# A gated cross-attention and mixture-of-experts block: VectorE's expert selection split over two slots, its one-hot products a slot later, TensorE's rank matmuls behind the queries

## What is computed

```python
x = x + tanh(g_xattn) * xattn(layernorm(x), ctx, mask, ...)
x = x + tanh(g_ffn) * ffn(layernorm(x), ...)
# in ffn, per token:
scores = sigmoid(h @ gate_w.T)                 # 32 experts
sc = scores + e_bias
group_scores = top_k(sc.reshape(T, 8, 4), 2)[0].sum(-1)
# the 4 best of 8 groups are kept, the scores of the others set to 0
masked = where(score_mask > 0, sc, 0.0)
topk_idx = top_k(masked, 6)[1]
topk_w = scores at topk_idx, / their sum, * 2.5
out = sum over the 6 experts of topk_w * relu2(h @ up[e].T) @ down[e].T
      + relu2(h @ shared_up.T) @ shared_down.T
```

## Time and profile before

| | us |
|---|---|
| median of 3 runs | 762.55 |
| lowest and highest | 761.95 to 765.81 |
| the profiled execution, its own time | 763.1 |
| its span in the trace | 761.3 |
| TensorE busy | 704.7 (93%) |
| VectorE busy | 521.1 (68%) |
| ScalarE busy | 454.3 (60%) |
| GpSimd busy | 490.4 (64%) |

### The profile page before, as it was taken

How to read it: one execution, slowest core, us unless ns; L and a number is a source line. 1 busy time by engine, 2 the same in 40 slices (tenths; PEclk the granted TensorE clock), 3 DMA queues, 4 the chain that set the end, 5 groups by cost and what they waited for, 6 DMA issues and landing times.

```text
span 761.3 us, 17715 instructions
## 1 busy us (share of the span) xinstructions
PE 704.7 (93%) x5360; PEld 600.2 (79%) x5360; DVE 521.1 (68%) x1782; ACT 454.3 (60%) x1299; POOL 490.4 (64%) x532
## 2 busy tenths in 40 slices
PE   5978898999899999889996999999999999999977
PEld 4867797888788888775672889988898878988865
DVE  0867578787778787876471445556578878888783
ACT  0267576778787878764414455567655665566730
POOL 1244442566666666578888857777777777777772
PEclk9999999999999999999999999999999999999999
DMA  8970000144222222435659566665699999999865
GB/s 310 376 226 2 1 3 1 67 143 150 92 90 91 90 92 95 155 134 201 220 184 285 166 202 213 189 186 185 206 322 320 324 319 339 313 332 340 263 213 164
DMA packets 78237, 144.72 MB, mean 190 GB/s; under 512 B 13750, under 2 KB 60097, under 8 KB 77120
## 3 DMA queue, kind: packets, MB, share of 16 engines
q1 hardware_dynamic: 51472, 67.46, 28.4%
q0 software_dynamic: 19968, 52.34, 18.6%
q10 hardware_dynamic: 6704, 23.80, 9.7%
HBM read 78.00 MB, written 69.73 MB: 194 GB/s over the span
## 4 chain that ended last, share of the span: by engine, by line
PE 50%; DVE 16%; POOL 12%; issue 5%; DMA 5%; ACT 5%; DVEq 5%; ACTq 1%; SPq 0%; POOLq 0%
PE ps L1427 10%; PE ps L1412 10%; POOL routed_rows L446 9%; PE ps L1400 5%; PE ps L1212 4%; PE ps L1222 4%; PE ps L1308 4%; DMA mid<-routed_rows 3%; ACT att L533 3%; PE ps L1166 3%; POOL bias_o L440 3%; PE ps L1112 2%; PE ps L1298 2%; PE ps L1199 2%; DMA picked<-in_mask 2%
## 5 line engine op out<-in xcount | busy, mean ns | idle before, releaser
L446 POOL DMA_INDIRECT routed_rows<-x_n,slots x120 | 120.1, 1001 | 64.7 <-issue 27.7
L483 POOL DMA_INDIRECT token_parts<-hid,place x112 | 114.2, 1020 | 45.1 <-issue 28.3
L629 ACT ACTIVATE att<-ps 128x512 f32<-128x512 f32 x106 | 63.3, 597 | 108.8 <-PE ps L1400 101.0
L1427 PE MATMUL ps<-big,att 128*128 x448 | 119.7, 390 | 8.9 <-ACT hid L653 3.3
L1412 PEld LDWEIGHTS ps<-att 128*128 128x128 f32 x848 | 112.2, 193 | 5.6
L1412 PE MATMUL ps<-att 128*128 128x128 f32 x848 | 112.6, 276 | 0.0
L1427 PEld LDWEIGHTS ps<-big,att 128*128 128x128 f32 x448 | 78.9, 191 | 29.3 <-issue 22.4
L533 ACT ACTIVATE att<-ps,nmax,rstd 128x154 f32<-128x154 f32 x176 | 82.0, 494 | 13.3 <-DVE nmax L758 13.1
L1212 PE MATMUL ps<-att,big 128*64 128x128 f32 x1024 | 70.7, 281 | 16.7 <-ACT att L550 11.7
L642 ACT ACTIVATE att<-big 128x256 f32 x224 | 80.2, 408 | 1.7 <-issue 0.8
L1212 PEld LDWEIGHTS ps<-att,big 128*64 128x64 f32 x1024 | 60.0, 138 | 24.4 <-ACT att L550 14.2
(11 more groups left out here) (254 smaller groups left out, 1439.1 us busy)
## 6 DMA issues: line engine op xcount, KB each, us to landing
mid<-routed_rows SPq DMA_DIRECT2D x224, 138.0 KB
big<-token_parts ACTq DMA_DIRECT2D x19, 768.0 KB, 6.9
x_n<-token_parts ACTq DMA_DIRECT2D x9, 768.0 KB
routed_rows<-pad_row SPq DMA_DIRECT2D x1, 4416.0 KB, 23.2
routed_rows<-pad_row SPq DMA_DIRECT2D x32, 138.0 KB, 2.8
x_all<-in_x SPq DMA_DIRECT2D x4, 1024.0 KB, 14.0
big<-in_x_t SPq DMA_DIRECT2D x4, 1024.0 KB, 16.1
big<-in_w_moe SPq DMA_DIRECT2D x2, 2048.0 KB, 11.4
```

The source lines that it names most:

```text
L446: nc.gpsimd.indirect_dma_start(rows, bass.IndirectOffsetOnAxis(ap=slots[:, t, k:k + 1], axis=0), normed(t), None).then_inc(s_sca[t // TB % ...
L483: nc.gpsimd.indirect_dma_start(parts, bass.IndirectOffsetOnAxis(ap=place[:, p // 2 % 8, p % 2 * 2 + j:p % 2 * 2 + j + 1], axis=0), y_sb[p ...
L629: A.activation(xt(p), ps[:, p % 2, :], ACT.Copy).then_inc(s_xts, 1)
L1427: ins = M(ps[:, 6 + p % 2, j * D:(j + 1) * D], h_t[:, p % 2, j * P:(j + 1) * P], w_exp[:, bass.ds(e, 1), 256:512].rearrange("p a n -> p (a ...
```

## The change

VectorE's selection is cut in two behind the removal of the group maxima. `router_top_groups` (the first half) stays in slot 4b+8 in front of `invert`. `router_select` (the second half, from `chosen` to `sel`) moves to slot 4b+9, behind that slot's maxima and its residual add, which comes ahead of it. `router_pick` (the products `hot` and `picked`) moves out of `router_slots` to slot 4b+10, behind that slot's maxima and ahead of its residual add. On TensorE `ranks` moves behind the remaining transposes and the queries. The last block's router, which runs behind the slots, keeps its order. No instruction is added or removed.

```diff
-            def router_select(b):
+            def router_top_groups():
                 for i in range(TB):
                     V.max(best[:, i, :], group_2[:, i, :])
...
                     V.match_replace(group_r[:, i, :], best[:, i, :], group_2[:, i, :], -2.0e38)
+
+            def router_select():
                 dve.drain()
                 V.tensor_tensor(chosen, group_r[:, :, 0:NG], group_2[:, :, 0:NG], ALU.not_equal)
...
+
+            def router_pick():
                 V.tensor_tensor(hot[:], key[:].unsqueeze(2).broadcast_to([P, TB, TOPK, NE]),
...
+                if T % 4 == 2 and T >= 10:
+                    router_pick()
                 if T % 4 == 0 and T >= 8:
                     residual_add(T - 3)
                     router_groups()
+                if T % 4 == 1 and T >= 9:
+                    residual_add(T - 3)
+                    router_select()
...
                 if T >= 3:
-                    if T % 4 or T < 8:
+                    if T % 4 > 1 or T < 8:
                         residual_add(T - 3)
...
                 if T % 4 == 0 and T >= 8:
-                    router_select((T - 8) // 4)
+                    router_top_groups()
...
-                if T % 4 == 1 and T >= 9:
-                    ranks((T - 9) // 4)
                 if 2 <= T < NT + 2:
                     probs_t(T - 2, 1)
                     probs_t(T - 2, 2)
...
                     ins = queries(T + 2)
...
+                if T % 4 == 1 and T >= 9:
+                    ranks((T - 9) // 4)
```

More of the change, by code:

```diff
@@ L978, in _ @@
             router_groups()
-            router_select(7)
+            router_top_groups()
+            router_select()
             add_shared(1, 0)
             router_slots(7)
+            router_pick()
             router_weights(7)
```

## The result

| | us |
|---|---|
| changed kernel, median of 4 runs | 777.66 (772.99 to 788.11) |
| kernel before, median of 4 runs | 763.14 (761.95 to 765.81) |
| ratio, with its 95% interval | 1.0123 (1.0074 to 1.0172) |
| the profiled execution of the changed kernel | 788.11, span 786.3 |
| TensorE, VectorE, ScalarE, GpSimd busy | 714.5, 520.6, 454.8, 487.1 |

By the ratio the changed kernel is 1.2% slower, some 9.4 us; the medians stand 14.5 us apart. Predicted were 4.2. The side was right, the size was not: 777.66 lies above the range of 761.5 to 770.5.

A forecast was written before the change was run, and what follows sets the result against it. Bound: a chain of waits, half of it TensorE's, through attention and router slots, GpSimd's scatters, then expert pairs. 3.7 + 1.2 - 0.7 = +4.2 us on 763.1 gives 767.3, or 766.8 on the median; range 761.5 to 770.5.

The forecast's parts named there:

- The six rounds: Rounds ending in slots 10 to 30: products on the path before the residual add, +3.7 us together, bounds +3.0 to +4.7.
- the rival of held products: In the six rounds, twelve moved products wait for GpSimd's scatters: 5.8 us more, 772.6 us; chance 0.05.
- a rival on slot 33: Slot 33: TensorE's clock holds behind the 2.7 us wait; +2.5 us in all, 765.0 us; chance 0.28.
- Slot 33 and the start of the pairs: Slot 33: selection stall and clock fall, +1.2 us (0 to 1.7); first expert pairs: less idle, -0.7 (-1.4 to +1.0).
- Rival B: Expert pairs: a good part of the loss arises there; named with the experiments, no chance given.
- The faster case: Six rounds: the products find cover between maxima and residual add, keeping 6.0 us; 756.5 us; chance 0.07.
- Rounds that cancel: Six rounds: shorter handovers take 3.0 us off, leaving +0.7 there and +1.2 in all; 763.8 us; chance 0.13.

The follow-up runs named there:

- third group's repeat: The changed kernel again without edit, on a chip where the kernel before took 768.71 us; 778.55 us, ratio 1.0146 to the kernel before.
- the transposes in the waits: Changed kernel plus 12 transposes of a constant ahead of the normed tiles' transposes in slots 11, 15, ... 31; 774.42 us, ratio 1.0080 to the kernel before.
- the two candidates: Changed kernel, selection ahead of slot 4b+9's residual add; one puts only the first product back, 764.22 us, the other both, 763.40 us.
- the second candidate: Changed kernel with both products back in slot 4b+9 and the selection ahead of that slot's residual add; 763.40 us, ratio 0.9960 to the kernel before.
- the run with the products back: Changed kernel with both products back in slot 4b+9, split selection and later ranks kept; 769.69 us, ratio 1.0013 to the kernel before.
- the products alone: Kernel before with only the two products moved behind slot 4b+10's maxima; 789.93 us, ratio 1.0278 to the kernel before.
- the ranks back: Changed kernel with the ranks back ahead of the remaining transposes and queries, selection still split; 794.58 us, ratio 1.0353 to the kernel before.
- the first group: The changed kernel unedited and three edits of it, on a chip with longer handovers; the unedited one took 831.28 us, ratio 1.0180.

## Why the prediction was off

The loss of the third group's repeat, up to the ninth pair, comes apart like this (VectorE's first instruction of that pair at 456.74 against 447.47, **9.3 us**):

- **The six rounds.** Predicted +3.7 (3.0 to 4.7). From slot 8's start to slot 31's normed tiles the kernel before takes 327.96 - 108.67 = 219.29 us; with the transposes in the waits, where no clock falls, it is 332.05 - 108.39 = 223.66. **+4.4**, inside the bounds; the transposes themselves may hold a little of it. Every step of slot 17 and 18 came within 0.17 us. That the products stand on the path was right: they took 0.95 and 0.96 in the mean of the six rounds, as before, with GpSimd scattering beside them in five, so the rival of held products fell. The Trainium skill (SBUF — State Buffer, section Who interferes with whom) has a VectorE instruction with two SBUF inputs contend with a GpSimd instruction that reads SBUF. The products show nothing of it, not even `hot`, which in five of the rounds starts while a scatter runs. The scatters do: one that starts under `hot` takes 1.10 us instead of 0.96.
- **The clock in the rounds.** This is the step that failed: the sum puts TensorE's clock in the six rounds at nothing, without a reason of its own. All that the prediction says of it stands in a rival on slot 33: "Idle stretches of 1.6 us in the rounds left no mark". That is so of the kernel before, whose waits for ScalarE's copies were up to 1.59, but it was no bound for six new waits of 1.8 us, each with a second one of 1.0 us two slots ahead. Three of the six are followed by a fall, with 3.37, 3.52 and 3.52 us for the projection instead of 1.89: **+4.7**, where the sum had nothing. This term alone takes 766.8 to 771.5, out of the range. I had priced the same fall at 1.7 us in slot 33 from the earlier trace rows.
- **Slot 33 and the start of the pairs.** Predicted +1.2 - 0.7 = +0.5. The stall was 2.73 (predicted 2.7), the fall cost 1.4 (1.7), and scatter 144 waited 1.99 us. From scatter 123 to scatter 144 the repeat took 32.1 us (340.81 to 372.90), the kernel before 30.7: +1.4 on GpSimd's chain, where +1.2 was forecast. What is left of the 9.3 us for slot 33 and the start of the pairs together is 9.3 - 4.4 - 4.7 = **+0.2**, so the pairs' start gave back about 1.2 (predicted 0.7).
- **The rest of the way.** The ratio of the first comparison, 1.0123, is 9.4 us of 763, what the ninth pair shows; the medians there are 14.5 us apart, and the repeat's profile ends 14.4 us behind that of the kernel before, 5.1 of them arising behind the ninth pair. The profiled execution of the change was 25 us above that of the kernel before; 3.1 of it had arisen by slot 8, before the first moved instruction, 9.5 up to the ninth pair, and the other 12 behind it. Rival B would put these to the change. From the ninth pair to the end of the span the first profile of the kernel before took 313.8 us and its repeat 321.6, the repeat of the change 318.9 between them, and the two candidates, which end the slots early, 316.3 and 312.7. The disturbed profile of the change took 326.2, 4.6 beyond the longer one of the kernel before. So the change is not needed to explain most of it; whether it adds some was not shown, and about 5 us of the difference of the medians stay open with it.
- **The rivals.** The faster case was refuted by its own test: TensorE waited at the normed tiles. Rounds that cancel needed 3.0 us less than the sum; they came out 0.7 longer. That the clock might hold in slot 33 was no idle thought: it held there in the third group's run with transposes, behind the same 2.73 us.

## What to carry to other kernels

Moving work off one wait pays only if its new place has cover for the engine that ends the round: here 2.06 us of products left a place that was half free for one that was not, and the maxima's lead (1.4 us in slot 18) went into a new wait of TensorE. When a sum makes TensorE wait longer than it did, give each such wait a clock term with both ends, zero and the full fall, and let the range hold their number; a wait that left no mark before is no bound for the next. And put the work that another engine queues behind (here the selection) ahead of work that nobody waits for yet (the residual add). That one exchange is all that parts the second candidate from the run with the products back: from the start of slot 8, slot 31's normed tiles came 2.8 us sooner and slot 33's stall was gone. The ratios, 0.9960 and 1.0013 in two groups, touch at the ends of their intervals, so as a gain in time it is likely and not shown.

## What the runs showed of the hardware

The length of a wait did not decide whether the clock fell. Behind 1.7 to 1.8 us at the normed tiles it fell in three of six rounds of the changed kernel, in the same three in both profiles, in all six with the products alone, and with the ranks back it stayed at full speed in all six of them, though six waits of 3.5 us for `sel` lay ahead; behind one of these it fell, and behind five not (and again behind the seventh, 3.39 us in slot 33). Behind 2.73 us in slot 33 it fell in both profiles of the change and with the products back, and stayed in the third group's run with transposes. Behind 1.68 us for ScalarE's copies it fell in slot 30 and held in slot 10 with the products back, and the other way round in the second candidate. In the changed kernel's slot 11 it even stayed behind 2.44 us:

```profile
143.32 1.30 PE L1248 MATMUL ps<-cst,x_n 128*128 128x128 f32 x8 [2.44 <-DVE x_n L824]
144.46 1.89 PE L1233 MATMUL ps<-hid,big 128*128 128x256 f32 x8
```

In the changed kernel each fall cost 1.4 to 1.7 us. What does decide was not settled by these runs. The Trainium skill (TensorE: Matmul & The Clock Gate, section Part 1: The HAM clock gate) says that the activity window runs free of the kernel, and that the moment at which the clock changes therefore depends on where in it the work lands. Equal waits with unequal results agree with that, and no run here shows it.

The chip of the first group gave the kernel before 817 us instead of 763 to 769, with the same code. In the changed kernel's slots there the clock was at 1.00 almost everywhere, and what was longer were the handovers between engines. On this chip the change lost 1.8% instead of 1.2 to 1.5%, with intervals that overlap.
